# Gated cross-attention and a mixture of experts on one core: all projection weights loaded at once, the key weights split on GpSimd

## The reference, cut to what matters

```
x (16, 256, 256), ctx_1024 (16, 77, 256), Wq (256, 1024), Wkv (256, 2048), Wo (1024, 256)   # float32

l  = layer_norm(_layernorm(x), ln2)          # 256 latent rows of a batch, normed twice
xc = layer_norm(ctx_1024, ln1)               # 77 context rows
q  = l @ Wq
k, v = split(concatenate([xc, l]) @ Wkv)     # 16 heads of 64
w  = softmax(q k^T / 8)                      # 256 x 333 for each head
x  = x + tanh(g_xattn) * ((w v) @ Wo)
x  = x + tanh(g_ffn) * (shared convolution block + top 2 of 16 experts)(_layernorm(x))
```

## Time and profile before

| | |
|---|---|
| median of three runs | 1365.5 us (1364.32 to 1367.94) |
| the profiled execution | 1364.59 us, its span 1362.8 us |
| mean granted TensorE clock | 0.981 |
| busy, share of the span | PE 92%, DVE 66%, ACT 47%, POOL 54% |
| DMA | 70.90 MB, mean 52 GB/s |

### The profile page before, as it was taken

How to read it: one execution, slowest core, us unless ns; L and a number is a source line. 1 busy time by engine, 2 the same in 40 slices (tenths; PEclk the granted TensorE clock), 3 DMA queues, 4 the chain that set the end, 5 groups by cost and what they waited for, 6 DMA issues and landing times. The chain is left out here.

```text
span 1362.8 us, 28186 instructions
## 1 busy us (share of the span) xinstructions
PE 1257.7 (92%) x8982; PEld 1023.9 (75%) x8982; DVE 900.1 (66%) x2710; ACT 636.2 (47%) x1958; POOL 738.3 (54%) x894
## 2 busy tenths in 40 slices
PE   1899999999999999999999999999999886999996
PEld 1688888878787877778778878788888774877764
DVE  4566677776776777676767676777666564455464
ACT  2555555454554454555454545554555421333332
POOL 1655645666555666566565646565656412454444
PEclk9999999999999999999999999999999987999998
DMA  4950000000000000000000000000000601345656
GB/s 129 296 161 4 3 1 4 17 4 17 7 13 13 9 11 10 12 9 15 7 19 2 19 3 20 1 19 1 17 2 17 182 8 49 112 126 163 201 175 201
DMA packets 61823, 70.90 MB, mean 52 GB/s; under 512 B 7056, under 2 KB 56160, under 8 KB 61664
## 3 DMA queue, kind: packets, MB, share of 16 engines
q1 hardware_dynamic: 54464, 49.96, 12.7%
q0 software_dynamic: 6912, 18.95, 3.8%
q10 hardware_dynamic: 288, 0.00, 0.0%
HBM read 35.19 MB, written 33.70 MB: 51 GB/s over the span
## 5 line engine op out<-in xcount | busy, mean ns | idle before, releaser
L1087 POOL TENSOR_SCALAR probs<-probs,inv_sum 128x333 f32<-128x333 f32 x384 | 425.4, 1123 | 0.0
L1137 ACT ACTIVATE probs<-st,neg_max 128x333 f32<-128x333 f32 x512 | 268.8, 538 | 270.8 <-DVE neg_max L1276 270.8
L1084 POOL TENSOR_TENSOR probs<-probs,inv_sum 128x333 f32<-128x333 f32 x128 | 94.7, 740 | 403.4 <-DVE inv_sum L1287 403.1
L1276 DVE TENSOR_REDUCE neg_max<-st 128x2 f32<-128x666 f32 x256 | 205.9, 846 | 133.1 <-PE st L1369 133.1
L1353 PE MATMUL st<-ident,probs 128*128 128x128 f32 (+1 forms) x1536 | 204.1, 273 | 1.1 <-POOL probs L1087 1.1
L1388 PE MATMUL ov<-PT,V 128*64 128x256 f32 (+1 forms) x1536 | 197.5, 392 | 0.0
L1353 PEld LDWEIGHTS st<-ident,probs 128*128 128x128 f32 (+1 forms) x1536 | 182.8, 143 | 17.9 <-POOL probs L1087 1.4
L1323 PE MATMUL pj<-wkv,lT 128*128 128x512 f32 (+1 forms) x576 | 158.5, 411 | 16.1 <-DVE Q_hl L1296 15.9
L1369 PE MATMUL st<-K_hl,Q_hl 64*128 64x334 f32 x1536 | 153.1, 331 | 18.3 <-issue 8.9
L1308 DVE COPY PT<-st 128x512 f32<-128x512 f32 x256 | 163.8, 682 | 0.8 <-PE st L1353 0.8
L1388 PEld LDWEIGHTS ov<-PT,V 128*64 128x64 f32 (+1 forms) x1536 | 100.2, 138 | 64.7 <-issue 28.5
(11 more groups left out here) (175 smaller groups left out, 1729.6 us busy)
## 6 DMA issues: line engine op xcount, KB each, us to landing
slots_x<-zeros SPq DMA_DIRECT2D x10, 1032.0 KB, 13.5
V<-slots_x SPq DMA_DIRECT2D x80, 129.0 KB
yg<-routed_y SPq DMA_DIRECT2D x32, 256.0 KB, 3.2
out<-X SPq DMA_DIRECT2D x32, 128.0 KB
stage<-in_L_xattn_Wkv SPq DMA_DIRECT2D x4, 512.0 KB, 4.0
X<-in_x SPq DMA_DIRECT2D x2, 1024.0 KB, 13.9
w_gu<-in_L_ffn_expert_gate_w SPq DMA_DIRECT2D x2, 960.0 KB, 9.3
w_gu<-in_L_ffn_expert_up_w SPq DMA_DIRECT2D x2, 960.0 KB, 10.3
```

Of the source, the lines that this page charges most:

```text
L1084: pool.tensor_tensor(probs[:, v, 0, 0:SKV], probs[:, v, 0, 0:SKV], inv_sum[:, v, 0:1].to_broadcast([P, SKV]), ALU.mult).then_inc(normed, 1)
L1087: pool.tensor_scalar(probs[:, v, i, 0:SKV], probs[:, v, i, 0:SKV], inv_sum[:, v, i:i + 1], None, ALU.mult).then_inc(normed, 1)
L1137: nc.scalar.activation(probs[:, v, i, 0:SKV], st_bank(i)[:, 0:SKV], ACT.Exp, bias=neg_max[:, v, i:i + 1], accum_out=sums[:, v, i:i + 1]).t ...
L1276: nc.vector.tensor_reduce(neg_max[:, v, 2 * i:2 * i + 2], st[i][:, :, 0:SKV], AX.X, ALU.max, negate=True).then_inc(maxed, 1)
```

## The change

SP loads 256 KB of x first (two tiles, batch 0) and the other two tiles later under a semaphore of their own. Each of the six weight pieces has its own stage and its own semaphore: Wq stays in the two old slots and is issued from ScalarE's queue ahead of the gate loads, the key half lies in the room of the turned probabilities, the value half in the room of the probabilities. SP issues the four Wkv pieces without a wait, then x's second part, the second context, and Wo after VectorE's two splits of Wq. GpSimd makes the low parts of the two key pieces after its `inv_std`; VectorE makes those of Wq and of the value half. VectorE's split of the first Wq piece moves between the second and the third part of the norm, the wait for the norm vectors behind the splits of Wq. TensorE waits for `key_lo` before the first key projection and for four low parts of VectorE before the first value projection.

```diff
--- before.py
+++ after.py
@@ -629,6 +629,10 @@
     PT = sb("PT", [P, 2, NKT, 2 * SQ])
     OT_hl = sb("OT_hl", [P, 2, 2, SQ], F32R)
 
+    turned_room = PT[:].rearrange("p a k q -> p (a k q)")
+    probs_room = probs[:].rearrange("p a i k -> p (a i k)")
+    w_stage = [stage[:, 0, :], stage[:, 1, :], turned_room[:, 0:INNER], turned_room[:, INNER:2 * INNER],
+               probs_room[:, 0:INNER], probs_room[:, INNER:2 * INNER]]
     conv_raw = stage[:, 0, 0:D * kept.KS_].rearrange("p (d k) -> p d k", k=kept.KS_)
     h_stats = sb("h_stats", [P, QT, 6])
     h_now = sb("h_now", [P, QT, 2])
@@ -669,12 +673,14 @@
     ctx_used = sem("ctx_used")
     ln_in = sem("ln_in")
     gate_in = sem("gate_in")
-    w_in = [sem("w_in0"), sem("w_in1")]
+    w_in = [sem(f"w_in{i}") for i in range(3 * KD)]
     wo_in = [sem("wo_in0"), sem("wo_in1")]
     wo_hi = sem("wo_hi")
     wo_split = sem("wo_split")
     w_hi = sem("w_hi")
     w_lo = sem("w_lo")
+    x_second = sem("x_second")
+    key_lo = sem("key_lo")
     consts = sem("consts")
     tables = sem("tables")
     gates = sem("gates")
@@ -1001,22 +1007,18 @@
     def sync(sp):
         sp.dma_start(ctx_t[0:SC, :], ctx_in[0]).then_inc(ctx_loaded, 16)
         rows = x.rearrange("b (q p) d -> p (b q) d", p=P)
-        first = slice(0, 2 * QT)
-        sp.dma_start(X[:, first, :], rows[:, first, :]).then_inc(x_in, 16)
+        sp.dma_start(X[:, 0:QT, :], rows[:, 0:QT, :]).then_inc(x_in, 16)
         for i, v in enumerate((ln1_g, ln1_b, ln2_g, ln2_b)):
             sp.dma_start(gb[:, i, :], v.rearrange("(k p) -> p k", p=P),
                          allow_slow_non_contiguous=True).then_inc(ln_in, 16)
-        pieces = [(Wq, k, 0) for k in range(KD)] + [(Wkv, k, n) for n in range(2) for k in range(KD)]
-        for i, (w, k, n) in enumerate(pieces):
-            if i == 2:
-                sp.wait_ge(ctx_used, 1)
-                sp.dma_start(ctx_t[0:SC, :], ctx_in[1]).then_inc(ctx_loaded, 16)
-            if i >= 2:
-                sp.wait_ge(w_lo, i - 1)
-            sp.dma_start(stage[:, i % 2, :], w[k * P:(k + 1) * P, n * INNER:(n + 1) * INNER]
-                         ).then_inc(w_in[i % 2], 16)
+        for i in range(KD, 3 * KD):
+            k, n = i % KD, i // KD - 1
+            sp.dma_start(w_stage[i], Wkv[k * P:(k + 1) * P, n * INNER:(n + 1) * INNER]).then_inc(w_in[i], 16)
+        sp.dma_start(X[:, QT:2 * QT, :], rows[:, QT:2 * QT, :]).then_inc(x_second, 16)
+        sp.wait_ge(ctx_used, 1)
+        sp.dma_start(ctx_t[0:SC, :], ctx_in[1]).then_inc(ctx_loaded, 16)
         for i in range(2):
-            sp.wait_ge(w_lo, len(pieces) - 1 + i)
+            sp.wait_ge(w_lo, i + 1)
             sp.dma_start(wo_stage(i), Wo.rearrange("(q p) d -> p q d", p=P)[:, wo_half(i), :]
                          ).then_inc(wo_in[i], 16)
         sp.wait_ge(zeros_set, 3)
@@ -1112,17 +1114,23 @@
 
         inv_std(0, 0, QT + 1)
         inv_std(0, 1, QT)
+        for k in range(KD):
+            pool.wait_ge(w_hi, KD + k + 1)
+            pool.tensor_tensor(wkv[:, 1, k, 0:INNER], w_stage[KD + k], wkv[:, 0, k, 0:INNER].bitcast(F32),
+                               ALU.subtract).then_inc(key_lo, 1)
         return pipeline(pool, step)
 
     def scalar(act):
+        for k in range(KD):
+            act.dma_start(w_stage[k], Wq[k * P:(k + 1) * P, :]).then_inc(w_in[k], 16)
         act.dma_start(tanh_g[:, 0:1], g_xattn.partition_broadcast(P)).then_inc(gate_in, 16)
         act.dma_start(tanh_g[:, 1:2], g_ffn.partition_broadcast(P)).then_inc(gate_in, 16)
 
         hi = [wq[:, 0, k, :] for k in range(KD)] + \
              [wkv[:, 0, k, n * INNER:(n + 1) * INNER] for n in range(2) for k in range(KD)]
         for i, w in enumerate(hi):
-            act.wait_ge(w_in[i % 2], 16 * (i // 2 + 1))
-            nc.scalar.activation(w, stage[:, i % 2, :], ACT.Copy).then_inc(w_hi, 1)
+            act.wait_ge(w_in[i], 16)
+            nc.scalar.activation(w, w_stage[i], ACT.Copy).then_inc(w_hi, 1)
         act.wait_ge(gate_in, 32)
         nc.scalar.activation(tanh_g[:], tanh_g[:], ACT.Tanh).then_inc(gates, 1)
 
@@ -1186,6 +1194,8 @@
             C = 2 + KD
             if part == 0:
                 dve.wait_ge(ctx_loaded, 16 * (j + 1))
+                if isinstance(j, int) and j == 1:
+                    dve.wait_ge(x_second, 16)
                 if isinstance(j, int) and j == 2:
                     dve.wait_ge(x_rest, 16 * 3)
                 for t in range(QT):
@@ -1237,10 +1247,8 @@
             tt(lT[:, v, 1, k, :], lT32[:, k, :], lT[:, v, 0, k, :].bitcast(F32), ALU.subtract).then_inc(lt_ready, 1)
 
         dve.wait_ge(x_in, 16)
-        dve.wait_ge(ln_in, 16 * 4)
-        for part in range(3):
+        for part in range(2):
             layer_norm(0, part)
-
 
         lo = [(wq, k, 0) for k in range(KD)] + [(wkv, k, n) for n in range(2) for k in range(KD)]
 
@@ -1249,13 +1257,16 @@
                 w, k, n = lo[i]
                 dve.wait_ge(w_hi, i + 1)
                 cols = slice(n * INNER, (n + 1) * INNER)
-                tt(w[:, 1, k, cols], stage[:, i % 2, :], w[:, 0, k, cols].bitcast(F32), ALU.subtract).then_inc(w_lo, 1)
-
-        split_weights(range(2))
+                tt(w[:, 1, k, cols], w_stage[i], w[:, 0, k, cols].bitcast(F32), ALU.subtract).then_inc(w_lo, 1)
+
+        split_weights(range(1))
+        layer_norm(0, 2)
+        split_weights(range(1, KD))
+        dve.wait_ge(ln_in, 16 * 4)
         for k in range(KD):
             transposed(0, 0, k)
             split_rows(0, 0, k, 0)
-        split_weights(range(2, 3 * KD))
+        split_weights(range(2 * KD, 3 * KD))
         dve.wait_ge(gates, 1)
 
         def step(bb, u, has):
@@ -1398,7 +1409,7 @@
                 split3(bank[:, 0:SQ], lambda a, k: wq[:, a, k, p * P:(p + 1) * P],
                        lambda a, k: lT[:, w, a, k, 0:SQ]).then_inc(pj_full, 1)
                 if first:
-                    pe.wait_ge(w_lo, 2 * KD)
+                    pe.wait_ge(key_lo, KD)
                 _, bank, free, value = filled("K", PAIRS, bb, u)
                 pe.wait_ge(free, value)
                 split3(bank[:, 0:SKVE], lambda a, k: wkv[:, a, k, p * P:(p + 1) * P],
@@ -1411,7 +1422,7 @@
                 kt, half = V_STEPS[p] % NKT, V_STEPS[p] // NKT
                 k0, kn = KT[kt]
                 if first:
-                    pe.wait_ge(w_lo, 3 * KD)
+                    pe.wait_ge(w_lo, 2 * KD)
                 _, bank, free, value = filled("V", len(V_STEPS), bb, len(V_STEPS) * (u // PAIRS) + V_STEPS[p])
                 pe.wait_ge(free, value)
                 split3(bank[0:kn, :], lambda a, k: lT[:, w, a, k, k0:k0 + kn],
```

## The result

The changed kernel takes 1359.37 us (median of five runs, 1356.18 to 1362.39) against 1367.35 us for the kernel before in the same comparison (1364.32 to 1367.94). The ratio is 0.9948, with a 95% interval of 0.9925 to 0.9972: by it the kernel is 7.1 us faster (3.8 to 10.3), by the two medians 8.0. The forecast was 8.5 us and 1357.0, with a range of 1351.5 to 1361.5. The measured time lies in that range and the forecast gain in that interval; the way there was not quite the one described.

The account below looks back on a forecast made before the run. TensorE bounds attention once running, so the start's gain counts: 3.35 + 8.0 + 1.25 = 12.6 us, less 4.1 for the engine clash, is 8.5 us, giving 1357.0 by the median; range 1351.5 to 1361.5.

Parts of the forecast that it names:

- the two-stage waits: Wkv loads waiting for splits to free two stages; removing them brings the value projection 8.0 us nearer the columns' end.
- The clash of the two engines: At the start, GpSimd's key splits and VectorE's two-operand SBUF instructions hold each other for whole lengths; 4.1 us lost.
- the rival of a late start and held rows: x lands at 8.5 (2 us lost) or rows wait for both key splits (5.6 lost); 1359.0, both 1360.5; chance 0.15.
- the clash as worked out: Main case: root operations, split 1 and the cast held, 4.1 us lost; 1357.0, own range 1354.5 to 1359.5; chance 0.50.
- Start of the norm: VectorE's first statistics start at 6.6 us instead of 8.85, as x's first load is halved; gain 2.25 us.
- near the first, as Wq leads: Choice of 6.6 us for x's landing, between bounds 6.0 (no Wq in the way) and 8.5 (all of it).
- the second rival: Start does not come forward, or row normalizations wait for both key splits; 1359.0 for one, 1360.5 for both; chance 0.15.
- the working without a clash: VectorE's chain from statistics to transposed columns with nothing held: columns end at 18.25 against 21.58, 3.35 us gained.
- TensorE's pace: First value projection runs at the faster clock level after TensorE's unbroken work; gain 1.25 us, bounds 0 and 1.25.
- Queues, the covers of ScalarE and GpSimd, Wo: Weight copies and key splits finish 2.6 and 2.4 us before needed; reordered queues and earlier Wo cost 0.
- The slower rival (the clock): Seven or eight more half-clock drops after TensorE's pauses eat the gain, giving 1370; chance 0.03.

Follow-up runs that it names:

- the repeat: The changed kernel run and profiled once more, unedited; median 1361.3 us over seven runs, ratio to the kernel before 0.9961.
- the kernel with all three: Changed kernel, but SP issues Wq behind x, VectorE makes all low parts, step 0's next-batch statistics come last; median 1355.7 us, ratio 0.9910.

## Why the prediction was right, and which of its steps were not

The direction and the size were right, and for the main reason given: the two-stage waits were worth 8 us between columns and value projection. Measured are 4.06 us from the columns' end to the value projection, against 12.25 before; the prediction had 4.25. The clash of the two engines was forecast from two small rows and is there at full length. That the number came so near is in part luck: of the mechanism at the start, what came is nearer to the rival of a late start and held rows, which was given a chance of 0.15 and priced at 1359.0 for one and 1360.5 for both, than to the clash as worked out, whose range (1354.5 to 1359.5) holds the measured 1359.4 only just.

- **Start of the norm: mis-sized.** 6.6 us was forecast, 7.73 measured (7.6 to 8.2 in the five other profiles with Wq ahead). The step that failed is "near the first, as Wq leads": of Wq's 2.5 us, 1.8 fell on x and not into its latency, as the run with Wq behind x shows. The bound without Wq in the way, 6.0, is right (5.87 and 6.04 in the two such runs). Cost: 1.1 us.
- **The clash: right in kind, other instructions.** The forecast let the row normalizations run beside a key split and made split 1 and the cast wait. Measured, the rows wait, both of them, for both key splits, and split 1 and the cast meet nobody. That was the second half of the second rival, "against it: the rows read one SBUF tile with two scalars", and this reason was wrong. The forecast loss was 4.1 us. Measured, the columns end 16.17 us behind the start, where the working without a clash has 11.65: 4.5, or 5.2 in the repeat. Of this the run with VectorE's keys leaves 0.9 for the root operations that split 0 holds (forecast 1.05).
- **TensorE's pace: chance, not a gain.** 1.25 us was taken off. The first value projection ran at the upper level in the first profile (1.62) and for the most part in one other (1.84), at the lower (2.90) in the six others with a changed start; and in the two where it was fast the second was slow (2.71, 2.23). In the first profile 1.28 - 1.05 = 0.2 us are left.
- **Sum.** 1.1 + 0.4 + 1.05, less the 0.2 us by which the stretch from columns to value projection was shorter than forecast, are 2.4 us, and 8.5 - 2.4 = 6.1; the gain of the first profile at the first output projection is 5.9. In the repeat it is 5.0.
- **What comes through.** 5.9 and 5.0 stand beside 7.1 us (interval 3.8 to 10.3) and 5.3 us (3.4 to 7.2) by the ratios of the two sets. The 1357.0 were reckoned from 1365.5, and the kernel before measured 1367.35 in the comparison: from there 8.5 us would give 1358.9, and 1359.4 came. The middle of the interval is kinder to the forecast than the chain of the start, which says 5 to 6.
- **Queues, the covers of ScalarE and GpSimd, Wo:** right; no weight landing and no key split was waited for. The last copy of ScalarE ends at 17.3, forecast near 15.6, still 6.5 us before it is needed.
- **The slower rival (the clock)** did not decide, but its mechanism is one part of what makes profiles of one kernel differ: half-clock stretches behind the pauses at the loop's turns.

The change's own idea for GpSimd does not pay: VectorE does two key splits in 2.35 us, and with GpSimd doing them in 4.7 the value projection is 1.4 us later.

## What to carry to other kernels

Before work is moved from VectorE to GpSimd, list what VectorE runs meanwhile: of what ran beside a key split here, only the scalings that read PSUM kept their own pace. A gap in which one engine waits for another's small operation is no room for a long instruction, if that instruction holds the small operation up. Of transfers issued at once, what is needed first must be ahead on every queue: here 1 MB on another queue cost x 1.8 us. And before a loss between two profiles is explained, take a second profile of both kernels.

## What the runs showed of the hardware

- A row normalization (128x256, SBUF to SBUF, two scalars) is held by a GpSimd subtraction for its whole length: 2.43 us instead of 0.41, twice in a row. The two engines took turns: one row normalization ended 0.1 to 0.2 us behind each key split. The Trainium skill (SBUF — State Buffer, Who interferes with whom) counts `tensor_scalar` among the operations that can take both of VectorE's ports and so contend with GpSimd; the trace agrees, and the prediction had overlooked it.
- The hold goes both ways and goes by order: VectorE's 1.19 us split stretched a GpSimd addition of two elements from 0.19 to 1.08, and in the fastest kernel its root operation from 0.70 to 1.75.
- GpSimd's memsets and iotas, which only write, also go with longer row normalizations: 0.7 us more in the repeat, and 1.13 for two instead of 0.73 in four profiles where GpSimd makes its constants beside them. It is not always so: in the kernel with all three, the rows keep their 0.73 beside the same memsets, and the memsets are the longer ones (0.31 instead of 0.12).
- 256 KB of x landed 6.3 us after its issue with 1 MB on the other queue ahead of it, and 4.5 us after it without (VectorE's start 1.8 us earlier). Twice the bytes, with nothing large ahead, took 6.0 in one profile of the kernel before and 5.4 in the other.
